# Graph attention: four buffers of keys and values for three, and the queries of one chain fetched in each batch

## What is computed

```python
q = (h @ Wq + bq).reshape(n, HD, HEADS) * scaling
k = (h @ Wk + bk).reshape(n, HD, HEADS)
v = (h @ Wv + bv).reshape(n, HD, HEADS)
s = jnp.einsum('edh,edh->eh', q[rows], k[cols])
m = jax.ops.segment_max(s, rows, num_segments=n)
e = jnp.exp(s - m[rows])
z = jax.ops.segment_sum(e, rows, num_segments=n)
attn = e / z[rows]
out = jax.ops.segment_sum(attn[:, None, :] * v[cols], rows, num_segments=n)
return out.reshape(n, -1) @ Wo + bo
```

## Time and profile before

| what | value |
|---|---|
| median of 3 runs | 5195.24 us (5195.18 to 5197.65) |
| the profiled execution's own time | 5205.05 us |
| its span in the profile | 5203.3 us |
| VectorE busy | 3332.6 us (64%) |
| GpSimd busy | 3544.3 us (68%) |
| TensorE busy | 1137.2 us (22%) |
| ScalarE busy | 435.2 us (8%) |
| stretch of the attention pass | 3727 to 5090 us of the span |

### The profile page before, as it was taken

One profiled execution on the slowest core, in us unless ns is written; L12 is line 12 of the kernel. 1 busy time (PEld: TensorE's weight loads), 2 busy tenths in 40 slices (PEclk: granted clock), 3 DMA queues, 4 the chain that ended last, 5 costly groups with the idle time before them and its releaser, 6 DMA issues. The chain is left out here.

```text
span 5203.3 us, 23830 instructions
## 1 busy us (share of the span) xinstructions
PE 1137.2 (22%) x4119; PEld 731.7 (14%) x4119; DVE 3332.6 (64%) x6972; ACT 435.2 (8%) x1091; POOL 3544.3 (68%) x3661
## 2 busy tenths in 40 slices
PE   4333321116233211015222200038500000000005
PEld 3222211114111100014111100025300000000003
DVE  4778777765444444436355433346499999999996
ACT  4000000002000000003000000014200000000001
POOL 0777777755777777765777777753477777777764
PEclk9555555558555555557555555569755555555557
DMA  4566566644666666656666666643477777777773
GB/s 132 187 209 203 202 211 202 202 166 128 209 215 216 212 205 206 208 171 194 215 202 211 219 204 211 205 160 118 160 233 228 232 228 234 228 235 229 233 215 113
DMA packets 331366, 1039.45 MB, mean 200 GB/s; under 512 B 71129, under 2 KB 132198, under 8 KB 297808
## 3 DMA queue, kind: packets, MB, share of 16 engines
q0 software_dynamic: 206896, 619.92, 39.7%
q1 hardware_dynamic: 124320, 418.01, 22.0%
HBM read 649.96 MB, written 388.11 MB: 200 GB/s over the span
## 5 line engine op out<-in xcount | busy, mean ns | idle before, releaser
L489 POOL DMA_INDIRECT G<-tab,ix x2349 | 2316.4, 986 | 725.5 <-issue 676.8
L519 DVE SCALAR_TENSOR_TENSOR G<-G,reset 128x256 f32<-128x256 f32 x2349 | 1036.8, 478 | 1438.4 <-DMA G<-tab,ix 1438.2
L1499 POOL DMA_INDIRECT kv<-kvtab,dst_ix x936 | 885.2, 946 | 352.2 <-issue 277.5
L611 PE MATMUL tail<-ident,h 128*128 128x128 f32 x294 | 95.3, 427 | 1060.7 <-DVE U L580 1041.5
L1545 DVE TENSOR_TENSOR kv<-kv,wide 128x3072 f32<-128x3072 f32 x78 | 261.1, 3347 | 101.2 <-DMA kv<-kvtab,dst_ix 101.2
L1686 PE MATMUL trio<-ident,state 128*128 128x128 f32 x6 | 2.0, 430 | 1377.3 <-DVEq L1708 1377.3
L1561 DVE TENSOR_REDUCE s<-kv 128x96 f32<-128x3072 f32 x78 | 261.0, 3346 | 0.0
L876 PE MATMUL trio<-hot 128*128 128x196 bf16 x783 | 143.7, 368 | 503.6 <-DVE hot L855 503.6
L1314 POOL DMA_INDIRECT pool<-hist,nix x147 | 139.1, 946 | 115.2 <-DVE nix L1320 79.3
L611 PEld LDWEIGHTS tail<-ident,h 128*128 128x128 f32 x294 | 42.0, 200 | 1167.6 <-issue 1146.9
L594 ACT ACTIVATE hT<-tail 128x256 f32<-128x256 f32 x147 | 56.3, 383 | 1672.2 <-PE tail L611 1672.2
(11 more groups left out here) (350 smaller groups left out, 3554.6 us busy)
## 6 DMA issues: line engine op xcount, KB each, us to landing
hist<-G SPq DMA_DIRECT2D x261, 1152.0 KB, 4.9
G<-tab,ix POOLq DMA_INDIRECT x2349, 3.0
ahist<-state SPq DMA_DIRECT2D x78, 408.0 KB, 4.1
tab<-o SPq DMA_DIRECT2D x147, 128.0 KB, 1.9
kv<-kvtab,dst_ix POOLq DMA_INDIRECT x936, 3.8
h<-tab SPq DMA_DIRECT2D x98, 128.0 KB, 5.1
G<-tab SPq DMA_DIRECT2D x98, 128.0 KB, 2.4
kvtab<-okv SPq DMA_DIRECT2D x49, 256.0 KB, 2.0
```

Source lines behind the costliest of these rows:

```text
L489: g.indirect_dma_start(G[b][:, k, :], None, tab, bass.IndirectOffsetOnAxis(ix[:, b, k:k + 1], 0)).then_inc(s_eg[b].sem, 16)
L519: ins = v.scalar_tensor_tensor(out=G[b][:, k, :], in0=before, scalar=reset[:, at:at + 1], in1=G[b][:, k, :], op0=ALU.add, op1=ALU.max)
L611: t = pe.transpose(self.turned[:, k * P:(k + 1) * P], self.h[:, b, k * P:(k + 1) * P], ident[:, :])
L1499: g.indirect_dma_start(kvs[b][:, k, :], None, kvtab, bass.IndirectOffsetOnAxis(dst_ix[:, at:at + 1], 0)).then_inc(s_eg[b].sem, 16)
```

## The change

The pass gets KB = 4 buffers of keys and values, used in turn by batch number, each with a semaphore of its own, and QB = 3 buffers of queries. The queries of window i + 1 are fetched in the three batches of window i, those of one chain behind the 12 transfers of each batch. To make room, `src_ix` and `reset` become one tensor `pass_lists`, which `pairs` takes in the attention pass, and `w_q`, `w_kv` and their biases go into the inner scope that closes before the pass.

```diff
-        src_ix = sb(top, "src_ix", [P, CH + 2 * J], I32)
+        pass_lists = sb(top, "pass_lists", [P, CH + 2 * J + CH])
+        src_ix, reset = pass_lists[:, 0:CH + 2 * J].bitcast(I32), pass_lists[:, CH + 2 * J:CH + 2 * J + CH]
...
-        reset = sb(top, "reset", [P, CH])
...
         def attention_pass(st, state, empty):
-            kvs = [sb(st, f"kv{b}", [P, SLOT * R, KV]) for b in range(UB)]
-            qs = [sb(st, f"q{b}", [P, R, T, D]) for b in range(2)]
+            KB, QB = 4, 3
+            kvs = [sb(st, f"kv{b}", [P, SLOT * R, KV]) for b in range(KB)]
+            qs = [sb(st, f"q{b}", [P, R, T, D]) for b in range(QB)]
...
-            pairs = sb(st, "pairs", [P, 2, R, D])
+            pairs = pass_lists[:, 0:2 * R * D].rearrange("p (a r f) -> p a r f", a=2, r=R)
...
+                    def queries(window, r):
+                        if window < WINDOWS:
+                            at = r * WINDOWS + window
+                            g.indirect_dma_start(qs[window % QB][:, r, :, :].rearrange("p t f -> p (t f)"), None, qtab_flat,
+                                                 bass.IndirectOffsetOnAxis(win_ix[:, at:at + 1], 0)).then_inc(s_query[window % QB], 16)
+
                     def gather(i, b):
                         n = i * UB + b
-                        if b == 0:
-                            if i >= 2:
-                                g.wait_ge(c_passed, i)
+                        if n == 0:
                             for r in range(R):
-                                at = r * WINDOWS + i
-                                g.indirect_dma_start(qs[i % 2][:, r, :, :].rearrange("p t f -> p (t f)"), None, qtab_flat,
-                                                     bass.IndirectOffsetOnAxis(win_ix[:, at:at + 1], 0)).then_inc(s_query[i % 2], 16)
-                        if i:
-                            g.wait_ge(c_taken.sem, c_taken.of(i - 1, b, UB))
+                                queries(0, r)
+                        if n >= KB:
+                            g.wait_ge(c_taken.sem, c_taken.base + n - KB + 1)
                         for k in range(R * SLOT):
                             at = (k % R * NBA + n) * SLOT + k // R
-                            g.indirect_dma_start(kvs[b][:, k, :], None, kvtab, bass.IndirectOffsetOnAxis(dst_ix[:, at:at + 1], 0)).then_inc(s_eg[b].sem, 16)
+                            g.indirect_dma_start(kvs[n % KB][:, k, :], None, kvtab, bass.IndirectOffsetOnAxis(dst_ix[:, at:at + 1], 0)).then_inc(s_kv[n % KB], 16)
+                        if i + 1 >= QB:
+                            g.wait_ge(c_passed, 1 + i + 1 - QB + 1)
+                        queries(i + 1, b)
...
-                        v.wait_ge(s_eg[b].sem, s_eg[b].base + (i * (16 * GATHERS) + 16 * GATHERS))
+                        v.wait_ge(s_kv[(i * UB + b) % KB], ((i * UB + b) // KB + 1) * (16 * GATHERS))
...
-            w_q, w_o = sb(l1, "w_q", [P, KC, D]), sb(l1, "w_o", [P, KC, D])
-            w_kv = sb(l1, "w_kv", [P, KC, 2 * D])
-            v_q, v_o, v_kv = sb(l1, "v_q", [P, D]), sb(l1, "v_o", [P, D]), sb(l1, "v_kv", [P, 2 * D])
+            w_o, v_o = sb(l1, "w_o", [P, KC, D]), sb(l1, "v_o", [P, D])
             later = [(w_o[:, :, :], chunks(wo)), (v_o[:, :], rows(bo))]
             with scope() as t:
+                w_q, w_kv = sb(t, "w_q", [P, KC, D]), sb(t, "w_kv", [P, KC, 2 * D])
+                v_q, v_kv = sb(t, "v_q", [P, D]), sb(t, "v_kv", [P, 2 * D])
```

More of the change, by code:

```diff
@@ L1462, in attention_pass @@
             z_row = sb(st, "z_row", [P, R, HEADS])
-            pairs = sb(st, "pairs", [P, 2, R, D])
+            pairs = pass_lists[:, 0:2 * R * D].rearrange("p (a r f) -> p a r f", a=2, r=R)
             c_query, c_scored, c_passed = sem("att_query"), sem("att_scored"), sem("att_passed")
-            s_query = [sem(f"att_q{b}") for b in range(2)]
+            s_query = [sem(f"att_q{b}") for b in range(QB)]
+            s_kv = [sem(f"att_kv{b}") for b in range(KB)]
             WINDOWS = NBA // T
@@ L1527, in pass_on @@
                             return
-                        q = qs[i % 2]
+                        q = qs[i % QB]
                         v.wait_ge(c_query, times(i, b, 1) + 1)
@@ L1536, in multiply @@
                     def multiply(i, b):
-                        keys = kvs[b][:, :, 0:D].rearrange("p (e r) f -> p e r f", r=R)
+                        keys = kvs[(i * UB + b) % KB][:, :, 0:D].rearrange("p (e r) f -> p e r f", r=R)
                         if b == 0:
@@ L1550, in stage @@
                                 v.wait_ge(c_e.sem, c_e.of(i, b, UB))
-                            vals, by_slot = kvs[b][:, :, D:KV], wts[b][:, 0:SLOT, :, :].rearrange("p e r h -> p (e r) h")
+                            vals, by_slot = kvs[(i * UB + b) % KB][:, :, D:KV], wts[b][:, 0:SLOT, :, :].rearrange("p e r h -> p (e r) h")
                             part = slice(half * HALF, (half + 1) * HALF)
@@ L1561, in add_up @@
                         keep("sums", i * UB + b, v.tensor_reduce(scores().rearrange("p e r h -> p (e r) h"),
-                                                                 kvs[b][:, :, 0:D].rearrange("p k (h d) -> p k h d", h=HEADS), AX.X, ALU.add))
+                                                                 kvs[(i * UB + b) % KB][:, :, 0:D].rearrange("p k (h d) -> p k h d", h=HEADS), AX.X, ALU.add))
                     def before(i, b):
@@ L1587, in pair @@
                         v.tensor_tensor(pairs[:, :, :, :].rearrange("p a r f -> p (a r) f"), first,
-                                        kvs[b][:, HALF:2 * HALF, D:KV], ALU.add).then_inc(c_taken.sem, 1)
+                                        kvs[(i * UB + b) % KB][:, HALF:2 * HALF, D:KV], ALU.add).then_inc(c_taken.sem, 1)
                     def maximum(i, b):
@@ L1625, in bring @@
                         if b == 0:
-                            a.wait_ge(s_query[i % 2], (i // 2 + 1) * (16 * R))
+                            a.wait_ge(s_query[i % QB], (i // QB + 1) * (16 * R))
                         if is_first(i, b):
@@ L1630, in bring @@
                             a.wait_ge(c_scored, times(i, b - 1, 1))
-                        a.activation(query, qs[i % 2][:, :, 0, :], ACT.Copy).then_inc(c_query, 1)
+                        a.activation(query, qs[i % QB][:, :, 0, :], ACT.Copy).then_inc(c_query, 1)
                     def expo(i, b):
@@ L1650, in attention_pass @@
             for b in range(UB):
-                s_eg[b].close(NBA // UB * 16 * GATHERS)
                 s_hs[b].close(NBA // UB * 16)
```

## The result

| what | before | with the change |
|---|---|---|
| median | 5195.21 us (4 runs, 5193.92 to 5197.65) | 5139.56 us (4 runs: 5130.77, 5138.92, 5140.19, 5140.63) |
| profiled execution | 5205.05 us, span 5203.3 | 5140.19 us, span 5138.4 |

The ratio is 0.9888 (95% interval 0.9872 to 0.9904): 1.1% faster. The median is 2.6 us above the range of the prediction, 5126 to 5137 us. The profiled execution was forecast at 5140.6 us and took 5140.19 us.

The account below looks back on a forecast made before the run. The prediction took the loop through three key and value buffers as the bound. 66.3 us from the windows, less 1.2 at the start and 0.6 for rounding and last turns, gave 64.5 us: 5195.24 - 64.5 = 5130.7 us, range 5126 to 5137.

Parts of the forecast that it names:

- GpSimd's stream becomes the bound, with no stall: Attention pass: GpSimd never stalls, issues every 1.2502 us, and a window falls from 51.41 to 48.76 us; chance 0.86.
- The fourth buffer gives 66.3 us, the spread queries nothing: Attention pass: 25 steady windows each save 2.65 us, together 66.3 us; moving the queries behind each batch costs nothing inside windows.
- The start loses 1.2 us: Start of the pass: second batch stands behind 16 issues, not 15; second multiply moves from 3763.84 to about 3765.1, losing 1.2 us.
- VectorE's waits for data stay at 0.3 us a window: Attention pass: VectorE still waits for keys and values, once or twice a window, some 0.3 us together.
- New waits, room and scopes at 0: GpSimd's waits on `c_passed` cost 0 (1 us for the range); moved tensors and weight scopes 0, with 2 us either side.
- The transfers carry it: Transfers in the pass: DMA share rises from 0.77 to 0.81, landing stays near 3.8 us; cost 0, at most 1.3 us.
- The rule on the shared port: VectorE operations with two SBUF inputs would block GpSimd's stream for their length in each batch; the forecast took no cost.
- the saving is taken from the median: Whole program: the 64.5 us forecast on the profiled execution is subtracted from the median, 5195.24 us, giving 5130.7 us.
- the scatter of a median of few runs, which spread over 2.5 us: Whole program: run scatter of 2.5 us, used with the other bounds for the 8-in-10 range of 5126 to 5137 us.

Follow-up runs that it names:

- the fifth series: Follow-up on chip 12, kernel before 5201.89 us: fourth buffer without spread queries 5139.08 us (0.9875); spread queries with three key and value buffers 5165.79 us (0.9929).
- the third series: Follow-up on chip 7: unedited changed kernel 5135.36 us against 5199.77 us before (0.988); changed kernel with short queries 5135.28, double stores 5139.9, three more issues per window 5233.36 us.
- room alone: Kernel before with only the new memory layout and scopes, three key and value buffers, two of queries, queries in front of each window: 0.9998 and 0.9992 of it.
- the first measurement: The original measurement of the whole change against the kernel before: medians 5139.56 us against 5195.21 us, four runs each, ratio 0.9888.
- the repeat of the third series: The changed kernel run again without edit on chip 7, signals in time: 5135.36 us, 0.988 of the kernel before.
- the second series: Follow-up on chip 2, kernel before 5571.67 us: change 1.0024, fourth buffer alone 1.003, spread queries alone 1.0006; changed kernel without later query transfers 5493.15 against 5589.92 us.

## Why the prediction was right in the pass and missed the median

- **GpSimd's stream becomes the bound, with no stall**: shown. A window went from 51.41 to 48.68 us (forecast 48.76), and the last issue stands (4996.10 - 3728.72)/1013 = 1.2511 us for each issue after the first (forecast 1.2502). That three more issues in a window cost 98 us says the same by an experiment.
- **The fourth buffer gives 66.3 us, the spread queries nothing**: shown by the fifth series, 62.8 us for the buffer alone against 64.4 us for both in the third series; the difference is within the scatter, and the pass is as long in the traces of both. That the spread alone would give 36 us with three buffers was not in the prediction, and doesn't add to it.
- **The start loses 1.2 us**: from the first issue to the second multiply 37.6 us (3766.31 - 3728.72) and before 36.35 us (3763.84 - 3727.49).
- **VectorE's waits for data stay at 0.3 us a window**: 6.7 us in 1200 us, 0.27 us a window.
- **New waits, room and scopes at 0**: no wait on `c_passed` shows; room alone gave 0.9998 and 0.9992, both where signals were late. **The transfers carry it**: share 0.79 in a window (forecast 0.81), landing at 3.8 us.
- **The rule on the shared port** (the Trainium skill, SBUF — State Buffer, "Who interferes with whom"): what looks like its mark is in the trace, but it is tiny. The longest issue of a gather grew from 967 to 1048 ns and the longest `differ` (L1624) from 284 to 356 ns; the 45 gathers that start while a `differ` runs take 967 ns in the mean (before, 25 of them, 958 ns). All 936 gathers together take 885.9 us against 885.2 us. A push by the whole length of such an operation in each batch, which for `differ` alone would be 78 x 0.283 = 22 us, is not there.
- **The step that failed** is the one from the profiled execution to the median, "the saving is taken from the median", and in it the term "the scatter of a median of few runs, which spread over 2.5 us". The saving on the profiled executions was 64.9 us against 64.5 us forecast, but the medians of the first measurement lie 55.7 us apart, those of the third series 64.4 us. The term was mis-sized: nine runs of the kernel before spread over 11.0 us in the third series and nine over 18.4 us in the fifth, and its median was 5195.2, 5199.8 and 5201.9 us in the first measurement and these two. The three runs that I had lay close together, and at the low end, by chance. The changed kernel's median was 5139.6 and 5135.4 us, single runs 5130.77 to 5140.63 us. And that the profiled execution came within 0.4 us of its forecast of 5140.6 is luck in part: its pass began 1.2 us later than before and its rest behind the last multiply was 2.5 us shorter, 135.4 us against 137.9. In the traces most of the scatter comes from ahead of the pass. The first query issue stood at 3721.0 us in one profiled execution of the changed kernel and at 3728.7 us in another, while the pass took 1274.8 and 1274.3 us in them and the rest of the span 138.0 and 135.4 us. Already the last gather of the maximum passes stands at 3430.8 in the one and at 3438.8 in the other:

```profile
L489 POOL DMA_INDIRECT G<-tab,ix x2349: 942/946/2446, 127.5 to 3430.8; - x196
```

```profile
L489 POOL DMA_INDIRECT G<-tab,ix x2349: 942/946/1966, 127.7 to 3438.8; - x196
```

  The first is the repeat of the third series, the second the first measurement. So 8 us of scatter arise in stages ahead of the pass, between two executions of one and the same kernel. A forecast of a median has to be wide by that, by some 5 us to either side as an estimate from the five medians above, however well the stage is known. What makes the maximum passes scatter is open.

Where signals are late, the forecast of a gain doesn't hold. There VectorE is no longer within 0.34 us of GpSimd: with its late waits it needs more than GpSimd's stream, a fourth buffer can only let GpSimd run further ahead, and VectorE waits longer for late signals than before (157.2 against 119.1 us on three lines, 38 us more, against 28 us less of waiting for data). In the pass this is 1435.8 us (4000.0 to 5435.8) against 1422.0 us (4002.0 to 5424.0); some 4 us of the difference are not in these groups. The ten traces of the three series with late signals agree, those with queries left out set aside: with four buffers the three lines have 151.6 to 158.6 us and the pass takes 1429.6 to 1436.8 us, with three buffers 108.6 to 120.1 us and 1418.5 to 1422.0 us. So more late waiting with a fourth buffer is shown, and its reason isn't. An unbroken stream of GpSimd is not it, since GpSimd isn't unbroken there: the idle time before its gathers of keys and values is 430.4 us with the change and 432.1 us with room alone, against 285.1 us in the first measurement. Whether bytes or issues do it, and what makes signals late in some series and not in others on the same chip, stays open.

## What to carry to other kernels

When two engines each wait once for the other in a cycle, and each alone would need less than the cycle, count how long a buffer is taken from its first transfer to its release: if that is as long as the turns of all the buffers together (here 51.4 us for three), the loop through them is the bound, and one more buffer leaves the slower engine's own stream as the bound; the gain is the difference of the two. Take the saving from stage to stage of one trace, but the range of a median from many runs: three that agree within 2.5 us said nothing of a scatter of 19 us. The same change gave 1.2% where signals came in time and cost 0.2 to 0.3% where they came late; look whether short instructions that wait for their own engine's last result show idle time before judging a change.

## What was not expected of the hardware

- In three of five series, on chips 7, 2 and 4, all kernels took 7% longer, and an instruction could wait up to 4.42 us for the end of the one before it on its own engine, with ScalarE and GpSimd waiting likewise. In the other two, on chips 7 and 12, this never showed in a trace.
- An indirect gather costs GpSimd 0.946 us and 0.30 us of gap whether it brings 1 KB, 2 KB or 3 KB for each partition (medians 946 ns on all three lines).
- In the second series, with late signals, leaving out 69 query transfers gave 96.8 us, 1.4 us for each, more than the 1.25 us that an issue takes. The late waits on the three lines are 88.8 us less in it.
